# Three score buffers, the next head's queries one step earlier, and stores in the turn of their rows: cross-attention with an expert feed-forward layer on one Trainium2 core

## The reference, cut to what matters

```python
def _L0_xattn_ref(q, k, v, gamma):           # k and v are both the context
    qh = q.reshape(B, h, dq, Lq)
    kh = k.reshape(B, h, dq, Lk)
    vh = v.reshape(B, h, dv, Lk)
    qk = jnp.einsum('bhdq,bhdl->bhql', qh, kh) * scale
    sm = jax.nn.softmax(qk, axis=-1)
    ret = jnp.einsum('bhql,bhdl->bhdq', sm, vh)
    return gamma * ret.reshape(B, Dv, Lq)

def _L0_ffn_ref(x, U, V, W1, b1, W2, b2):
    h = jax.nn.relu(jnp.einsum('bsd,de->bse', x, W1) + b1)
    alpha = jax.nn.softmax(jnp.einsum('bse,ek->bsk', h, W2) + b2, axis=-1)
    vx = jnp.einsum('krd,bsd->bskr', V, x)
    uvx = jnp.einsum('kdr,bskr->bskd', U, vx)
    return jnp.einsum('bsk,bskd->bsd', alpha, uvx)

x = x + _L0_xattn_ref(_layernorm(x, axis=-1), ctx_2048, ctx_2048, L0_xattn_gamma)
x = x + _L0_ffn_ref(_layernorm(x, axis=-1), ...)
```

## Time and profile before

| | |
|---|---|
| runs | 1518.27, 1519.21, 1520.94 us (median 1519.21) |
| the profiled execution | 1515.66 us, its span 1513.9 us |
| PE busy | 1476.6 us, 98% of the span |
| DVE busy | 1078.9 us, 71% |
| ACT busy | 822.8 us, 54% |
| POOL busy | 753.7 us, 50% |
| DMA | 338.65 MB, 224 GB/s over the span |
| attention's last matmuls of scores | begin at 745.3 us |

### The profile page before, as it was taken

How to read it: one execution, slowest core, us unless ns; L and a number is a source line. 1 busy time by engine, 2 the same in 40 slices (tenths; PEclk the granted TensorE clock), 3 DMA queues, 4 the chain that set the end, 5 groups by cost and what they waited for, 6 DMA issues and landing times.

```text
span 1513.9 us, 20359 instructions
## 1 busy us (share of the span) xinstructions
PE 1476.6 (98%) x6176; PEld 1140.2 (75%) x6176; DVE 1078.9 (71%) x1303; ACT 822.8 (54%) x1262; POOL 753.7 (50%) x471
## 2 busy tenths in 40 slices
PE   5999999999999999999989999999999999999999
PEld 3777777777777777777767877778787887878877
DVE  7999999999999999999758646354564525545212
ACT  5888889889889888898763122111221212112110
POOL 2888988988889889888745201102011020200200
PEclk9999999999999999999999999999999999999999
DMA  5889999999999999998895563635537364463304
GB/s 163 256 276 296 290 283 289 288 289 297 292 282 297 291 290 295 280 292 269 260 362 177 187 205 117 229 123 194 196 116 245 121 203 162 143 218 125 112 1 139
DMA packets 144248, 338.65 MB, mean 224 GB/s; under 512 B 29440, under 2 KB 48896, under 8 KB 144192
## 3 DMA queue, kind: packets, MB, share of 16 engines
q1 hardware_dynamic: 126624, 290.31, 61.4%
q10 hardware_dynamic: 17568, 47.72, 9.2%
HBM read 136.36 MB, written 52.69 MB: 125 GB/s over the span
## 4 chain that ended last, share of the span: by engine, by line
PE 70%; DVE 11%; SPq 6%; issue 5%; DMA 4%; ACT 3%; ACTq 1%; POOL 0%; DVEq 0%; POOLq 0%
PE scores L1098 21%; PE scores L559 14%; PE attended L588 9%; PE attended L1147 9%; PE spare L1129 5%; PE scores L1129 5%; PE attended L591 4%; SPq L223 4%; DVE pb L633 3%; DVE neg_max L624 3%; DMA attended_rows<-att_out 2%; DMA pt<-pb 1%; PE scores L1113 1%; PE scores L1116 1%; ACT probs L435 1%
## 5 line engine op out<-in xcount | busy, mean ns | idle before, releaser
L345 POOL TENSOR_TENSOR pt_lo<-pt,pt_hi 128x512 fp32r<-128x512 f32 x254 | 478.8, 1897 | 98.4 <-ACT pt_hi L414 96.7
L435 ACT ACTIVATE probs<-scores,neg_max 128x1024 f32<-128x1024 f32 x256 | 285.4, 1115 | 87.5 <-DVE neg_max L624 82.0
L633 DVE STREAM_TRANSPOSE pb<-probs 128x1024 f32<-128x1024 f32 x256 | 315.8, 1234 | 11.4 <-DMA pt<-pb 5.8
L624 DVE TENSOR_REDUCE neg_max<-scores 128x1 f32<-128x1024 f32 x256 | 309.7, 1210 | 19.7 <-PE scores L559 18.8
L559 PE MATMUL scores<-k_hi,q_hi 128*128 128x512 f32 x512 | 210.9, 493 | 26.5 <-ACT probs L435 16.9
L414 ACT ACTIVATE pt_hi<-pt 128x512 fp32r<-128x512 f32 (+1 forms) x256 | 214.3, 837 | 7.0 <-DMA pt<-pb 7.0
L1044 ACT ACTIVATE hidden<-scores,b_col 128x512 f32<-128x512 f32 x64 | 44.1, 689 | 316.3 <-PE scores L1098 316.3
L993 POOL TENSOR_TENSOR rstd<-var_eps,minus_half 128x1 f32<-128x1 f32 x28 | 15.2, 550 | 397.8 <-DVE var_eps L1210 397.8
L1098 PE MATMUL scores<-nt_hi,w_hi 128*128 128x512 f32 x512 | 200.2, 391 | 1.3 <-DVE w_lo L1178 1.3
L1098 PE MATMUL scores<-nt_lo,w_hi 128*128 128x512 f32 x512 | 199.7, 390 | 0.0
L1098 PE MATMUL scores<-nt_hi,w_lo 128*128 128x512 f32 x512 | 199.4, 389 | 0.0
(11 more groups left out here) (103 smaller groups left out, 2599.1 us busy)
## 6 DMA issues: line engine op xcount, KB each, us to landing
pt<-pb SPq DMA_DIRECT2D x512, 256.0 KB, 5.2
attended_rows<-att_out SPq DMA_DIRECT2D x64, 256.0 KB, 5.4
result<-x SPq DMA_DIRECT2D x64, 256.0 KB, 4.3
out<-result SPq DMA_DIRECT2D x64, 256.0 KB, 3.0
k_raw<-in_ctx ACTq DMA_DIRECT2D x30, 512.0 KB, 5.3
x_raw<-in_x ACTq DMA_DIRECT2D x30, 512.0 KB, 6.4
first_n<-attended_rows SPq DMA_DIRECT2D x28, 512.0 KB, 4.0
gain_wide<-gains SPq DMA_DIRECT2D x28, 512.0 KB, 5.7
```

Source lines behind the costliest of these rows:

```text
L345: nc.gpsimd.tensor_tensor(pt_lo[2 * parity + half][:, :, keys, :], pt[2 * parity + half][:, :, keys, :], as_f32(hi[half][q][:]), ALU.subtr ...
L435: nc.scalar.activation(probs[j % 2][:], scores[j % 2][:], ACT.Exp, bias=neg_max[:, j:j + 1], accum_out=row_sum[b][:, j:j + 1]).then_inc(s_ ...
L624: nc.vector.tensor_reduce(neg_max[:, j:j + 1], scores[j % 2][:], AX_X, ALU.max, negate=True).then_inc(s_max, 1)
L633: nc.vector.transpose(pb[half][:, :, j % HALF, :], probs[j % 2][:]).then_inc(s_blocks, 1)
```

## The change

1. `scores` becomes three PSUM tiles of two banks each in place of two; the third takes the two banks that attention did not use (`spare`). Step s uses tile s mod 3, and PE waits for the exponentials of three steps ago, not of two. `spare` and `turned`, which the second half and the end of attention use, become names for the third tile's halves; the first two transpositions into it wait for the exponentials of step 254.
2. The next head's queries are made a step sooner: variance in step 2 (was 3), `q_scale` and `q_shift` in step 2 (was 3), `q` and `q_hi` in step 3 (was 4), `q_lo` in step 5 (was 6). To make room, `k_lo` goes to step 3 (was 2); x of the head after next is loaded in step 4 (was 5), its keys in step 5 (was 4).
3. Both attended halves of head h-2 are stored in the turn of head h, half 0 behind the first eight `pt<-pb` DMAs and half 1 behind the second.

No instruction that computes is added or taken away, and no DMA.

```diff
+    def scores_of(h, j, own_step):
+
+        return scores[(2 * (OWN_AT + own_step[1] if own_step else h) + j) % 3]
...
-            if not (known and h < 3):
-                store_attended(h - 3, 1)
             if last:
                 load_first(n, (0, 1))
+
+            if not (known and h < 2):
+                store_attended(h - 2, 0)
             if not first:
                 send_gain(h - 1, 1)
-            if last:
-                store_attended(h - 2, 0)
             gather(h, n, 0, parity)
-            if not (known and h < 2 or last):
-                store_attended(h - 2, 0)
+            if not (known and h < 2):
+                store_attended(h - 2, 1)
             send_gain(h, 0)
...
         send_gain(h - 1, 1)
-        store_attended(h - 3, 1)
         sp.wait_ge(s_gather[0], heads * GATHERS)
...
                 if j == 2 and not last:
+                    scale_of_queries(h + 1, 1 - parity)
+                if j == 3 and not last:
                     low_keys(h + 1, 1 - parity)
-                if j == 3 and not last:
-                    scale_of_queries(h + 1, 1 - parity)
...
                 if j == 4 and more:
+                    act.wait_ge(s_q32, h + 2)
+                    load_x(h + 2)
+                if j == 5 and more:
                     act.wait_ge(s_klo, h + 2)
                     load_k(h + 2)
-                if j == 5 and more:
-                    act.wait_ge(s_q32, h + 2)
-                    load_x(h + 2)
...
-                if j == 4 and not last:
+                if j == 3 and not last:
                     queries(h + 1, 1 - parity)
                     high_queries(h + 1, n + JB, 1 - parity)
...
-            if not (isinstance(s, int) and s < 2):
-                pe.wait_ge(s_exp, s - 1)
+            if not (isinstance(s, int) and s < 3):
+                pe.wait_ge(s_exp, s - 2)
...
             if u >= 2:
                 pe.wait_ge(s_lo, u - 1)
+            else:
+
+                pe.wait_ge(s_exp, heads * JB - 1)
...
-                if j == 3 and not last:
+                if j == 2 and not last:
                     dve.wait_ge(s_stat, h * 2 + 4)
...
-                if j == 3 and not last:
+                if j == 2 and not last:
                     variance(h + 1, 1 - parity)
-                if j == 6 and not last:
+                if j == 5 and not last:
                     low_queries(h + 1, 1 - parity)
...
-        scores = shared["scores"] = [psum(f"scores{b}", [P, 2 * BANK]) for b in range(2)]
-        spare = [psum(f"spare{b}", [P, 4, P]) for b in range(2)]
+        scores = shared["scores"] = [psum(f"scores{b}", [P, 2 * BANK]) for b in range(3)]
...
-        shared["turned"] = [tile[:] for tile in spare]
-        shared["spare"] = [tile[:].rearrange("p k n -> p (k n)") for tile in spare]
+        shared["spare"] = [scores[2][:, half] for half in halves]
+        shared["turned"] = [half.rearrange("p (k n) -> p k n", n=P) for half in shared["spare"]]
```

More of the change, by code:

```diff
@@ L429, in load_v_native, with exps @@
                          ).then_inc(s_vn_in, 16)
-        def exps(s, j, b):
+        def exps(s, j, b, scored):
             act.wait_ge(s_max, s + 1)
@@ L434, in exps @@
                 act.wait_ge(s_blocks, s - 1)
-            nc.scalar.activation(probs[j % 2][:], scores[j % 2][:], ACT.Exp, bias=neg_max[:, j:j + 1],
+            nc.scalar.activation(probs[j % 2][:], scored[:], ACT.Exp, bias=neg_max[:, j:j + 1],
                                  accum_out=row_sum[b][:, j:j + 1]).then_inc(s_exp, 1)
@@ L484, in slot @@
             for j in range(JB):
-                exps(n + j, j, parity)
+                exps(n + j, j, parity, scores_of(h, j, own_step))
                 if j == 3 and not first:
@@ L543, in tensor, with score_products @@
         mm = nc.tensor.matmul
-        def score_products(s, j, h, b):
-            if not (isinstance(s, int) and s < 2):
-                pe.wait_ge(s_exp, s - 1)
+        def score_products(s, j, h, b, scored):
+            if not (isinstance(s, int) and s < 3):
+                pe.wait_ge(s_exp, s - 2)
             queries = slice(j * P, (j + 1) * P)
@@ L558, in score_products @@
                 for c in range(2):
-                    last = mm(scores[j % 2][:, c * BANK:(c + 1) * BANK], q[b][:, queries],
+                    last = mm(scored[:, c * BANK:(c + 1) * BANK], q[b][:, queries],
                               k[b][:, c * BANK:(c + 1) * BANK], start=(i == 0), stop=(i == 2))
@@ L606, in slot @@
             for j in range(JB):
-                score_products(n + j, j, h, parity)
+                score_products(n + j, j, h, parity, scores_of(h, j, own_step))
                 attended_products(quarter_in(h, n, j, parity, LAG))
@@ L621, in vector, with maxima @@
     def vector(dve):
-        def maxima(s, j):
+        def maxima(s, j, scored):
             dve.wait_ge(s_scores, s + 1)
-            nc.vector.tensor_reduce(neg_max[:, j:j + 1], scores[j % 2][:], AX_X, ALU.max,
+            nc.vector.tensor_reduce(neg_max[:, j:j + 1], scored[:], AX_X, ALU.max,
                                     negate=True).then_inc(s_max, 1)
@@ L693, in slot @@
                     dve.wait_ge(s_own_stat, t * 2 + 2)
-                maxima(n + j, j)
-                if j == 3 and not last:
+                maxima(n + j, j, scores_of(h, j, own_step))
+                if j == 2 and not last:
                     dve.wait_ge(s_stat, h * 2 + 4)
```

## The result

The changed kernel takes 1557.87 us (median of four runs, 1556.76 to 1558.70) against 1520.08 for the kernel before in the same measurement (four runs): ratio 1.0255, interval 1.0239 to 1.0270. It is slower by 38 us. The profiled execution took 1556.76 us, its span 1555.0.

What follows compares the result with a forecast made beforehand. PE bounded the kernel before, at 22.69 us a plain head; DVE would after the change. 341.6 + 188.4 + 203.2 = 733.2 against 695.0 gave +38 us, 1519.21 + 38 = 1557 us; own range 1535 to 1570, widened to 1514 to 1570.

Steps and rivals of the forecast that it cites:

- a plain head: Heads 1 to 3 and 28 to 30, and two per round: DVE needs 24.4 us, above PE's 22.69; 14 make 341.6.
- Which comes first: POOL's 128x1024 pt_lo starts at T + 6.7, 0.2 us before q_lo at T + 6.89, so q_lo takes 3.3 us.
- Rivals A and B: Both have q_lo first. A: PE then waits for pt_lo, 1524, chance 0.14. B: pt_lo in time, 1510, chance 0.14.
- Rival C: Waits of 1 to 2 us a head lower PE's clock; price 5.7 us, 1525; chance 0.05.
- The rounds' heads 1 and 3: Eight heads where the product fills the gap behind step 4: 23.55 us each, between 22.7 and 24.4; together 188.4.
- Heads 4 and 5 of a round: Four of each, with side statistics, variance and a delayed gap's end: 48.8 + 2.0 us a pair, 203.2 in all.
- The sum: Thirty heads, between maxima of step 0 in heads 1 and 31: 733.2 us against 695.0, so +38 us.
- The third buffer at 0: PE gets a step further ahead, which wins nothing with DVE the bound: 0, with bounds 0 and -14.4 us.
- the stores at 0: ACT's 3.4 us of store waits go but bring nothing; at attention's end half a microsecond either way, 0 taken.
- The bound of 14.4 us: Thirty heads took 695.04 us against 30 x 22.69 = 680.7: all that a deeper buffer and earlier store can win.
- The 2.9 us a round: A loop round of six heads takes 139.03 us where 136.14 would do; the prediction called this PE idling.
- rival B: q_lo first and pt_lo in time: PE stays the bound, 3.4 + 6 = 9 us won, thus 1510; chance 0.14.

Runs made afterwards that it cites:

- the best version: The changed kernel with q_lo and the side task's product with the gains each put one transposition earlier on DVE: 1512.96 us, ratio 0.9961.
- `q_lo` first: The changed kernel with q_lo kept in step 5 but ahead of the transposition of step 4's probabilities: 1523.32 us, ratio 1.0029.
- the split: The changed kernel with POOL's low part of the last quarter (128x1024 pt_lo) made by two 128x512 instructions: 1541.76 us, ratio 1.0143.
- the version with the queries in their old slots: Three buffers, earlier stores, q_lo and the product ahead of their steps' transpositions, but queries placed as in the kernel before: 1516.54 us, ratio 0.9988.

## Why the prediction was right

The forecast was 1557, within 1535 to 1570; it came out at 1557.87. Step by step, with T = 730.40 + 1.21 = 731.61, the end of the maxima of step 3:

| step | predicted | head 29 of the changed kernel |
|---|---|---|
| exponentials of step 4 start | T + 4.49 | 736.12 = T + 4.51 |
| DVE waits for them | 1.2 | 1.21 |
| the 128x1024 `pt_lo` starts | T + 6.7 | 738.34 = T + 6.73 |
| `q_lo` starts | T + 6.89 | 738.50 = T + 6.89 |
| `q_lo` ends | T + 10.2 | 741.81 = T + 10.20 |
| a plain head | 24.4 | 24.31 (maxima to maxima) |

*Which comes first.* The lead of `pt_lo` over `q_lo`, 0.2 us by the working, was 0.16 to 0.19 in 25 of 30 heads; in the other five, four of them with the product, it was 0.49 to 1.19, and `q_lo` took 2.3 to 3.0 us. I gave two rivals 0.14 each because that is small against the roughness of POOL's spans. It was steady: both starts hang on the same ACT instructions (the exponentials, and `pt_hi` behind them), so that the difference of two chains does not spread as each of them does. Rivals A and B, for which `q_lo` had to come first, did not occur. Rival C did not either: the clock is 1.00.

*The rounds' heads 1 and 3* are the term that was mis-sized. I took 23.55, the middle between 22.7 and 24.4; they are 24.30, the upper bound. The product does fill the gap ahead of the transposition (it takes 1.08 us in the median, finding only the last 0.1 us of `k_lo`, and 0.2 to 1.2 of wait are left), and `q_lo` and `pt_lo` stay in the order that they have in plain heads. Where the wait is longer, `q_lo` starts later and takes less, and the head is 24.30 all the same, since `q_lo` ends by when `pt_lo` ends. The step that failed is "`q_lo` and `pt_lo` become ready within hundredths of each other": I had let the product take its 2.1 to 2.3 us of before, with a wait for POOL in it, where that wait was gone. That is 8 x 0.75 = 6 us too little. It could have been more: the product starts 0.04 to 0.07 us ahead of another 128x1024 `pt_lo`, the one before that which `q_lo` meets, and that `pt_lo` takes 3.3 to 3.4 us. In the version with `q_lo` alone ahead of its transposition the product starts 0.09 to 0.52 us behind such a `pt_lo`, takes 2.8 to 3.3 us, and the heads take over 25.

*Heads 4 and 5 of a round:* predicted 50.8 together, measured 25.07 + 25.78 = 50.85.

*The sum.* Thirty heads: predicted 733.2, measured 770.64 - 32.40 = 738.24, so +43.2, not +38. Of the 5.0 us more, 6.0 are heads 1 and 3, and the plain heads give back about 1. The span grew by 41.1 only. In the last head, whose step 5 makes no `q_lo` for a next one, the maxima of steps 0 to 7 take 18.4 us where they took 19.4; 0.9 us less passes between attention's last product and the first of the second half; and that half's products take 734.25 us where they took 734.53. I had 0 for all of this. That the median came so near to 1557 is luck in part: the changed kernel's profiled execution lies 1.1 us under its median, where the kernel before had 3.55, so that an error of 41.1 - 38 = 3 was covered by the other.

*The third buffer at 0, the stores at 0:* borne out in this kernel (1.0257 with the queries alone against 1.0255 with all three parts; 0.9995 for the stores alone). The bound of 14.4 us for what a buffer can win was not reached: the best version won 695.04 - 690.31 = 4.7. The 2.9 us a round that I called idle time of PE are what the round takes beyond six plain heads; by the earlier trace rows PE idles for 139.03 - 137.83 = 1.2 of it. In the prediction only rival B used the 2.9.

*Who waits for what.* PE busy for 92 to 94% of a plain head: 96%. "DVE never waits for PE's scores": 3.7 us in all of attention. But I said that PE would stand at full buffers, waiting for exponentials; it stands for `pt_lo` (63.6 and 32.3 us). My reading, which no run tests by itself, is that with three buffers it is far enough ahead in scores that the attended products, whose `pt_lo` follows ACT's and POOL's pace, stop it first. With two buffers it is the exponentials, as I had it. The time is DVE's in both.

The rule of the Trainium skill that the prediction weighed (SBUF — State Buffer, "Who interferes with whom") held in every run: issue order decided who blocked. A hold to POOL's very end would add 0.1 us a head; the rows say 0.1 less, as the trace of before did, and the rows decide.

## What to carry to other kernels

Before an instruction with two SBUF inputs is moved on VectorE, write down what GpSimd is running at the new place, which of the two starts first, and how much of GpSimd's instruction is left. A slot that is "free" by busy time can cost the whole length of a GpSimd instruction in each turn, and moving one of two such instructions may put the other into the same trap. Here both `q_lo` and the `pt_lo` that held it stood behind the same exponentials, and the cure was to put `q_lo` ahead of that wait.

In this kernel the deeper buffer paid only where the engine that fills it was the bound: with VectorE the bound it won nothing that can be told from nothing, and with TensorE the bound some 2 us in the old order (0.9986, at the edge of its interval) and some 6 in the best one.

## What the runs showed of the hardware

The hold is exact, and it works both ways. A profile shows it in the held instruction's own duration, not as a wait before it. In the traces of before, of the changed kernel, of the queries alone, of `q_lo` in step 6, of `q_lo` first, of the split, and of the best version, I took each `q_lo` and each product that began with over 0.15 us of a POOL instruction still to run: 217 in all. Each took its own time (1.18 us and 1.06 us) plus what POOL had left, less 0.04 to 0.11 us; for `q_lo` it is 0.09 or 0.10 in every one. The smallest lead with which POOL held DVE was 0.1 us in these, and 0.03 in the version with the queries in their old slots, where the product took 3.32 us. The other way about, a `pt_lo` that began during a `q_lo` or a product took its own time plus what DVE had left, less 0.11 to 0.17 us, even where it began only 0.02 us after DVE. So in these runs the first to start always had its whole instruction, and a lead of a few hundredths decided over 2 us.

POOL did not keep DVE out for longer than one instruction: in the split version DVE, waiting, got in between two POOL instructions that stood back to back. The same of DVE is not shown, since in attention no two of its instructions with two SBUF inputs follow each other.
